# A fused attention and feed-forward kernel: another order and another split of work in its opening

## The reference

```python
h = layernorm(x) * (1 + ca) + sa
q, k, v = h @ Wq.T, h @ Wk.T, h @ Wv.T       # 8 heads, 64 wide for q and k, 128 for v
q, k = rotary(q), rotary(k)                  # x * cos + rotate_half(x) * sin
o = ((q @ k.T) * D**-0.5 * decay_of_head * causal) @ v
o = (o - mean(o)) * rsqrt(var(o) + EPS) * gn_weight + gn_bias      # for each head and token
x = x + ga * ((o * silu(h @ Wg.T)) @ Wo.T)
h = layernorm(x) * (1 + cb) + sb
hp = h shifted by one token
r = sigmoid((mu_r * h + (1 - mu_r) * hp) @ W_r.T)
x = x + gb * r * (relu((mu_k * h + (1 - mu_k) * hp) @ W_k.T) ** 2 @ W_v.T)
```

## Time and profile before

| | |
|---|---|
| median of three runs | 754.27 us (754.24 to 754.61) |
| the profiled execution, its own time | 754.64 us |
| its span from first to last instruction | 752.8 us |
| PE busy | 737.0 us (98%) |
| DVE busy | 605.5 us (80%) |
| POOL busy | 587.6 us (78%) |
| ACT busy | 490.0 us (65%) |

### The profile page before, as it was taken

The page is one execution under the profiler, slowest core; times in us unless marked ns, Lnnn a source line. Parts: engine busy times, 40 slices in busy tenths (PEclk is TensorE's granted clock), DMA queues, the critical chain, the costliest instruction groups (busy, mean ns, idle before and its releaser), DMA issues.

```text
span 752.8 us, 29013 instructions
## 1 busy us (share of the span) xinstructions
PE 737.0 (98%) x12148; PEld 648.1 (86%) x12148; DVE 605.5 (80%) x1272; ACT 490.0 (65%) x953; POOL 587.6 (78%) x642
## 2 busy tenths in 40 slices
PE   6999999999999999999999999999999999999997
PEld 5778888888889889888888988888888988988886
DVE  6988687979888797987879798797988878787546
ACT  3576657566675766767676666756667576666665
POOL 1778778888789887898778888888878987787652
PEclk9999999999999999999999999999999999999999
DMA  9310000000011010111102011020101101001100
GB/s 326 105 38 17 17 17 13 20 17 16 23 30 37 10 44 17 24 37 30 30 10 50 13 27 31 14 47 17 30 23 31 34 13 30 16 10 30 24 15 29
DMA packets 56161, 25.67 MB, mean 34 GB/s; under 512 B 36184, under 2 KB 53856, under 8 KB 56032
## 3 DMA queue, kind: packets, MB, share of 16 engines
q1 hardware_dynamic: 55312, 23.02, 12.8%
q10 hardware_dynamic: 720, 0.80, 0.3%
HBM read 11.22 MB, written 4.20 MB: 20 GB/s over the span
## 4 chain that ended last, share of the span: by engine, by line
PE 93%; issue 2%; POOL 2%; ACT 1%; DVE 1%; DMA 0%; POOLq 0%; DVEq 0%
PE ring L309 53%; PE outs L309 15%; PE O_E L309 13%; PE ring L324 8%; PE O_O L309 3%; PE ring L354 2%; POOL y L1325 1%; ACT y L747 0%; POOL qT L1302 0%; DMA X<-in_x 0%; POOL ln_rstd L1274 0%; POOL gn_rstd L1318 0%; ACT normed L694 0%; ACT v L709 0%; ACT h2T L810 0%
## 5 line engine op out<-in xcount | busy, mean ns | idle before, releaser
L1325 POOL TENSOR_TENSOR y<-y,gate 128x512 f32<-128x512 f32 x123 | 158.9, 1309 | 35.6 <-ACT y L747 35.6
L709 ACT ACTIVATE v<-ring 64x512 f32<-64x512 f32 x128 | 76.1, 594 | 81.4 <-PE ring L309 80.6
L1308 POOL TENSOR_TENSOR rot_k<-rot_k,sin_k 128x256 f32<-128x256 f32 x128 | 106.4, 852 | 24.5 <-DVE sin_k L1028 24.5
L309 PEld LDWEIGHTS outs<-wo_gated,y 128*128 128x128 f32 x992 | 119.7, 192 | 6.7 <-POOL y L1325 2.3
L309 PE MATMUL outs<-wo_gated,y 128*128 128x128 f32 x992 | 121.8, 275 | 1.4 <-POOL y L1325 1.4
L1055 DVE TENSOR_REDUCE gn_sum<-N 128x4 f32<-128x512 f32 x118 | 75.5, 681 | 42.5 <-ACT N L735 42.5
L1318 POOL TENSOR_TENSOR gn_rstd<-gn_var,minus_half 128x8 f32<-128x8 f32 x64 | 105.4, 1646 | 5.0
L1302 POOL TENSOR_TENSOR qT<-qT,swapped 128x512 f32<-128x512 f32 x64 | 82.8, 1294 | 29.1 <-DVE swapped L1011 29.1
L1035 DVE TENSOR_TENSOR A<-ring,consts 128x256 f32<-128x256 f32 x128 | 47.9, 415 | 60.0 <-PE ring L309 60.0
L747 ACT ACTIVATE y<-ring,gn 128x512 f32<-128x512 f32 x126 | 90.9, 776 | 5.1 <-PE ring L324 5.1
L717 ACT ACTIVATE kT<-ring 128x512 f32<-128x512 f32 x64 | 38.3, 598 | 77.7 <-PE ring L324 77.7
(11 more groups left out here) (172 smaller groups left out, 2092.0 us busy)
## 6 DMA issues: line engine op xcount, KB each, us to landing
k_odd<-rot_k SPq DMA_DIRECT2D x128, 64.0 KB, 2.3
X<-in_x SPq DMA_DIRECT2D x16, 256.0 KB, 4.0
out<-X SPq DMA_DIRECT2D x15, 256.0 KB, 2.5
key_tables<-in_const SPq DMA_DIRECT2D x7, 256.0 KB, 8.3
rotary_q<-in_const_q SPq DMA_DIRECT2D x2, 512.0 KB, 8.3
gates<-stored_rows SPq DMA_DIRECT2D x8, 128.0 KB, 3.1
N<-in_w_qkT SPq DMA_DIRECT2D x1, 512.0 KB, 4.7
N<-in_w_vT SPq DMA_DIRECT2D x1, 512.0 KB, 6.0
```

The costliest lines, as they stand in the source:

```text
L309: return e.matmul(o, lhsT, rhs, start=start, stop=stop, skip_group_check=True)
L709: done = e.activation(v[halves(half), i % 2, 1, :, :], by(PAIRS, bank_of["v", odd, i][halves(1 - half), :]), ACT.Copy)
L1308: done = e.tensor_tensor(turned[:, n, :, :], turned[:, n, :, :], sin[:, n, :, :], op)
L1325: e.tensor_tensor(y[:, n % NY, :], y[:, n % NY, :], gate[:, n % 2, :], ALU.mult).then_inc(sem["y"])
```

## The change

It touches the opening alone.

- The queries of group 0 get their rotated partners by a second projection. ACT copies the query weights with quarters exchanged into `mix_k` hi (`round_w_partners`), POOL makes the low part (`low_w_partners`), PE projects both (`project_q_pair`: six products a pair, the partners into the banks of the heads), DVE multiplies each and POOL subtracts. The four shuffles of group 0 go.
- The low part of the query and key weights is made by POOL, no longer by DVE. ACT scales the mean of the value weights, POOL takes it off in two halves (`centre_w_v(odd)`), ACT rounds each half and DVE makes the low part of each (`low_w_v(odd)`). `sum_w_v` stands on DVE ahead of the modulation columns.
- Group 1's statistics, deviation, apply, transpose and modulation stand later on all queues; so do `project_q(4)` and `project_q(5)` on PE, `rotate_q(5)` and `norm_stats(2, 0)` on DVE, `round_w_k` on ACT.
- The filler on PE is 4 narrow and 3 wide calls instead of 12, 15 and 7.
- On SyncE the exchange of chunk 0's keys stands behind the second table load, that of chunk 1 behind the next three loads, and the other loads behind them; `store_gates` comes before the exchange of chunk 2.

```diff
+            def project_q_pair(p):
+                cols = slice(p * P, (p + 1) * P)
+                bank = take_bank(("q", p), ("cos_q", p + 1))
...
+                split_matmul(bank[:, :], [wqk[s][:, cols] for s in ("hi", "lo")], h_parts(0))
+                at.wait_ge("w_partners_lo", 1)
+                at.wait_ge("sin_q", p - 1)
+                bank = bank_of["q_partners", p] = O[p % 2][:, :, :].rearrange("p n v -> p (n v)")
+                split_matmul(bank, [mix_k[s][:, cols] for s in ("hi", "lo")], h_parts(0)).then_inc(sem["proj_q"])
# PE's opening
             mod_columns()
             transpose_n(0, 0)
-            keep_busy(out_bank, 12, False)
-            project_q(0)
-            project_q(1)
-            project_q(2)
-            project_q(3)
+            keep_busy(out_bank, 4, False)
+            project_q_pair(0)
             project_k(0)
+            project_q_pair(1)
+            project_q_pair(2)
             project_v(0, 1)
-            keep_busy(out_bank, 15, True)
+            project_q_pair(3)
             project_v(0, 0)
-            transpose_n(1, 0)
             project_k(1)
-            keep_busy(out_bank, 7, True)
             transpose_k(0)
             project_v(1, 1)
+            keep_busy(out_bank, 3, True)
             scores(0)
             state(0)
-            project_q(4)
             mod_gates()
             project_v(1, 0)
             project_k(2)
+            transpose_n(1, 0)
             transpose_k(1)
             attend(0)
             scores(1)
             recall(0)
             state(1)
-            project_q(5)
+            project_q(4)
             project_v(2, 1)
             project_v(2, 0)
             project_k(3)
+            project_q(5)
             transpose_k(2)
# ACT's opening
             norm_apply(0, 0)
+            round_w_partners()
+            scale_v_mean()
             round_h(0)
-            split_w_v()
+            round_w_v(1)
+            round_w_v(0)
+            split_w_g()
+            copy_v(0, 1)
+            copy_kT(0)
+            copy_v(0, 0)
+            copy_v(1, 1)
             norm_apply(1, 0)
-            copy_v(0, 1)
-            copy_v(0, 0)
-            round_h(1)
-            copy_kT(0)
-            split_w_g()
-            copy_v(1, 1)
             copy_v(1, 0)
             copy_kT(1)
-            round_w_k()
+            round_h(1)
...
# DVE's functions and opening
+            def rotate_q_pair(p):
+                at.wait_ge("const_q0", 16)
+                at.wait_ge("proj_q", p + 1)
+                at.wait_ge("qT", p - 1)
+                e.tensor_tensor((turned, swapped)[p % 2][:, :], bank_of["q_partners", p], rotary_q[:, 1, 0:W], ALU.mult
+                                ).then_inc(sem["sin_q"])
+                e.tensor_tensor(qT[:, 0, p, :], bank_of["q", p][:, :], rotary_q[:, 0, 0:W], ALU.mult).then_inc(sem["cos_q"])
...
             norm_stats(0, 0)
-            split_w("w_qk", raw_qk, wqk)
+            sum_w_v()
             mod_columns()
             full_h(0)
-            sum_w_v()
             low_h(0)
-            centre_w_v()
+            rotate_q_pair(0)
+            rotate_k(0)
+            low_w_v(1)
+            rotate_q_pair(1)
+            low_w_v(0)
+            rotate_q_pair(2)
+            rotate_q_pair(3)
+            rotate_k(1)
             norm_stats(1, 0)
-            rotate_q(0)
-            split_w("w_v", raw_vc, wv)
-            rotate_q(1)
-            rotate_q(2)
-            rotate_k(0)
-            rotate_q(3)
-            full_h(1)
-            rotate_k(1)
-            norm_stats(2, 0)
             mask(0, 1)
             mask(0, 0)
             add_state(0)
+            rotate_k(2)
             mod_gates()
-            rotate_q(4)
-            rotate_k(2)
+            full_h(1)
             mask(1, 1)
             mask(1, 0)
             add_state(1)
-            rotate_q(5)
+            rotate_q(4)
             rotate_k(3)
             norm_heads(0, 0)
             mask(2, 1)
             mask(2, 0)
             norm_heads(0, 1)
+            rotate_q(5)
             add_state(2)
+            norm_stats(2, 0)
             rotate_q(6)
# POOL's functions and opening
+            def low_w_partners():
+                at.wait_ge("w_partners_hi", 1)
+                e.tensor_tensor(with_partners(mix_k["lo"][:, :]), with_partners(raw_qk[:, 0:H * D])[:, :, ::-1, :],
+                                with_partners(mix_k["hi"][:, :]).bitcast(F32), ALU.subtract).then_inc(sem["w_partners_lo"])
+            def centre_w_v(odd):
...
+                at.wait_ge("v_mean", 1)
+                e.tensor_tensor(by(PAIRS, raw_vc[:, cols]), by(PAIRS, raw_v[:, cols]),
+                                v_mean[:, heads].unsqueeze(2).broadcast_to([P, PAIRS, V]), ALU.subtract).then_inc(sem["w_v_centred"])
...
             norm_rstd(0, 0)
+            split_w_qk()
+            low_w_partners()
+            centre_w_v(1)
+            centre_w_v(0)
             rotate_q(0)
-            norm_rstd(1, 0)
+            rotate_k(0)
             rotate_q(1)
             rotate_q(2)
-            rotate_k(0)
             rotate_q(3)
+            rotate_k(1)
+            norm_rstd(1, 0)
+            rotate_k(2)
             low_h(1)
-            rotate_k(1)
             split_w_g()
             rotate_q(4)
-            rotate_k(2)
             head_rstd(0)
             rotate_k(3)
+            rotate_q(5)
             norm_rstd(2, 0)
-            rotate_q(5)
             head_rstd(1)
# SyncE
             load_tables(1)
+            load_tables(2)
+            swap_k(0)
             load_rotary(1)
-            for n in range(2, CB):
-                load_tables(n)
-                if n < NX:
-                    load_x(n)
-            swap_k(0)
+            load_x(2)
+            load_tables(3)
             swap_k(1)
+            for n in range(3, NX):
+                load_x(n)
+                load_tables(n + 1)
+            store_gates()
             swap_k(2)
-            store_gates()
             load_gates(0)
```

More of the change, by code:

```diff
@@ L55 @@
     "v_O", "v_mean", "v_sum", "w_ffn", "w_g", "w_g_hi", "w_g_lo", "w_k_hi", "w_k_lo",
-    "w_mod", "w_o", "w_qk", "w_qk_hi", "w_qk_lo", "w_v", "w_v_centred", "w_v_hi", "w_v_lo", "wffn_v",
+    "w_mod", "w_o", "w_qk", "w_qk_hi", "w_qk_lo", "w_v", "w_v_centred", "w_v_hi", "w_partners_hi", "w_partners_lo", "w_v_lo", "wffn_v",
     "wo_gated", "x0", "x1", "x2", "x3", "x4", "x5", "x6", "y", "zero_column",
@@ L266, in loaded, with with_partners @@
             return "x%d" % (g % NX), 16 * (g // NX + 1)
+        def with_partners(w):
+            return w.rearrange("c (a n q) -> c a n q", n=2, q=QUARTER)
         steps = range(-62, NCHUNK + 5)
@@ L428, in attend @@
                 heads = heads_of(i)
+                at.wait_ge("sin_q", PAIRS)
                 for eo in "EO":
@@ L675, in split_w, with scale_v_mean, round_w_v @@
                 e.activation(parts["hi"][:, :], raw_w, ACT.Copy).then_inc(sem[name + "_hi"])
-            def split_w_v():
-                at.wait_ge("w_v_centred", 1)
-                split_w("w_v", raw_vc, wv)
+            def scale_v_mean():
+                at.wait_ge("v_sum", 1)
+                e.activation(v_mean[:, :], v_mean[:, :], ACT.Copy, scale=1.0 / V).then_inc(sem["v_mean"])
+            def round_w_v(odd):
+                cols = slice(odd * W, (odd + 1) * W)
+                at.wait_ge("w_v_centred", 1 if odd else 2)
+                e.activation(wv["hi"][:, cols], raw_vc[:, cols], ACT.Copy).then_inc(sem["w_v_hi"])
             def split_w_g():
@@ L768, in round_w_k, with round_w_partners @@
                 e.activation(wk["hi"][:, :], wffn[:, 1, :], ACT.Copy).then_inc(sem["w_k_hi"])
+            def round_w_partners():
+                at.wait_ge("w_qk", 16)
+                e.activation(with_partners(mix_k["hi"][:, :]), with_partners(raw_qk[:, 0:H * D])[:, :, ::-1, :], ACT.Copy
+                             ).then_inc(sem["w_partners_hi"])
             def round_mix(g):
+                at.wait_ge("proj_q", PAIRS)
                 at.wait_ge("mix_k", g + 1)
@@ L850, in _ @@
             copy_kT(2)
+            round_w_k()
             scale_norm()
@@ L921, in _, with low_w_v @@
             at = Passed(e)
-            def split_w(name, raw_w, parts):
-                at.wait_ge(name + "_hi", 1)
-                e.tensor_tensor(parts["lo"][:, :], raw_w, parts["hi"][:, :].bitcast(F32), ALU.subtract
-                                ).then_inc(sem[name + "_lo"])
+            def low_w_v(odd):
+                cols = slice(odd * W, (odd + 1) * W)
+                at.wait_ge("w_v_hi", 1 if odd else 2)
+                e.tensor_tensor(wv["lo"][:, cols], raw_vc[:, cols], wv["hi"][:, cols].bitcast(F32), ALU.subtract
+                                ).then_inc(sem["w_v_lo"])
             def sum_w_v():
@@ L1004, in rotate_q @@
                 at.wait_ge("proj_q", m + 1)
-                at.wait_ge("swapped", m)
+                at.wait_ge("qT", PAIRS)
```

(12 more changed lines are left out.)

23 lines of the change are left out of this document (10 added, 13 removed).

## The result

The changed kernel takes 756.6 us (median of 20 runs, 755.0 to 758.03), the kernel before 754.25 on the same chip. The medians differ by 2.35 us. The ratio is 1.0027, 95% interval 1.0021 to 1.0033, which is 2.0 us: slower, and beyond the 0.2% that the prediction counts as no change. The profiled execution took 756.72 us with a span of 754.9 us, where 756.9 and 755.1 were predicted.

What follows compares the result with a forecast made beforehand. DVE up to rotate_q(6) was taken to bound the opening, PE carrying the shift on. 5.1 + 29.8 work + 12.7 holes = 47.6; +2.3 us taken on span 752.8 gives 755.1, median 756.6 us; range 752.9 to 757.9.

Steps and rivals of the forecast that it cites:

- To the first projection: Opening up to PE's first projection: sum_w_v waits for w_v, low_h(0) ends at 12.9, PE starts at 13.0 us, 1.0 earlier.
- low_h(0)'s turn: DVE's low_h(0), ready at 11.05, waits for POOL's centre_w_v(1) at the shared port until 12.2 us; bounds nothing to 1.4.
- the prediction's "only": SBUF port lock at low_h(0): stated as held against a DVE operation with two SBUF inputs only; no size for the word.
- The first pair: PE's first query pair: six products at twice 0.23, 2.7 us, done at 15.8; DVE starts rotate_q(0) at 15.9.
- the rise: PE's clock going from 1.2 to 2.4 GHz: expected after the first pair; if by 13.5 us, 1.2 us less.
- Where the lead goes: From scores(0) to rotate_q(6): 2.8 us lead spent through group 1's norm and head_rstd(0); rotate_q(6) at 47.8, +2.3 us taken.
- DVE's sums: Check over DVE up to rotate_q(6): 29.8 us of work and 12.7 of holes, 47.6 with the start at 5.1.
- Costs set at nothing: Opening: key exchange and later loads on SyncE's queue, gate stores and removed PE filler, each forecast to cost or gain nothing.
- B: Rival for the opening: one early delay absent, POOL's turn or the late clock; +1.2 to +1.4, 755.6 us; chance 0.27.
- D: Rival: faster, the lead at the scores survives, decided by head_rstd(0); 753.6 to 752.6, or 751.5 us; chance 0.15.
- E: Rival: PE's waits between 23 and 50 us let the clock drop again, +1.7 us, 758.3; chance 0.08.

Runs made afterwards that it cites:

- four-moves kernel: Changed kernel with head_rstd(0) directly behind low_h(1), six narrow fillers instead of four, centre_w_v's first half behind low_h(0), full_h(1) ahead of mod_gates: 753.02 us, ratio 0.9984.
- the version with the two moves: Changed kernel with only head_rstd(0) directly behind low_h(1) on POOL and full_h(1) ahead of mod_gates on DVE: 753.79 us, ratio 0.9995.
- the first experiment: Changed kernel with head_rstd(0) on POOL directly behind low_h(1), ahead of split_w_g and rotate_q(4): 755.34 us, ratio 1.0016.
- the version with the old transfers: Changed kernel with SyncE's transfers in the order of the kernel before, store_gates back behind swap_k(2): 756.76 us, ratio 1.0036.
- the two moves with 8 fillers: Changed kernel with head_rstd(0) directly behind low_h(1), full_h(1) ahead of mod_gates and eight narrow fillers instead of four: 753.67 us, ratio 0.9987.
- centre_w_v: Changed kernel in which POOL's first centre_w_v also waits for low_h(0): 756.27 us, ratio 1.0027.

## Why the prediction was right, and where it was not

The measured median is the predicted one, 756.6. The mechanism was right, but that the digits agree is in part luck: the shift of the span was put at 2.3 us and is 2.1, and the median was put 0.37 us below the profiled execution and lies 0.12 below it. The two errors cancel.

**To the first projection: right in kind, two terms too large.** sum_w_v waited for w_v until 7.98 (7.8 forecast), h was rounded at 11.08 (11.0). Splitting the exchanged weights took 1.27 us on POOL, not 1.4: the 16-element groups cost nothing (a plain subtraction of 512 elements takes 1.26). Taking off the mean in halves took 2.04 for both where nothing else was at the port (this is the four-moves kernel, POOL's queue), 1.0 each instead of 1.3, so with the broadcast operand it is cheaper than with a full one:

```profile
9.45 1.28 POOL L1315 TENSOR_TENSOR mix_k_lo<-N,mix_k_hi 128x512 fp32r<-128x512 f32 x1
11.83 2.04 POOL L1323 TENSOR_TENSOR N<-N,v_mean 128x512 f32<-128x512 f32 x2 [1.10 <-DVE hT_lo L1016]
```

So low_h(0)'s turn cost 0.64 us, not 1.2, and PE started at 12.58 instead of 13.0. That it was a turn is shown: with the order at the port settled, the same instruction took 0.69. By the Trainium skill, SBUF — State Buffer, section SBUF: two separate sides, the port pair is held for a whole instruction. The 1.11 to 1.44 us that low_h(0) took in every profile in which POOL came first agree, and so does the gates' operation beside low_h(1) in the version with the two moves: it ended at 33.40, 0.28 us after POOL's. The section also names DVE operations in a two-port mode, which the prediction's "only" leaves out; nothing here rests on that.

**The first pair: right in the sum, the clock longer low than forecast.** The pair was to be done at 15.8, DVE to start at 15.9 after 3.1 us; it was 15.59 after 3.15. But the rise was forecast behind the pair, and the products stayed 0.43 apart to 17.4 us, over five more of them. That cost little, as DVE, not PE, set the pace then: scores(0) came at 25.42, with 25.6 forecast.

**Where the lead goes: right step by step.** full_h(1) ended at 33.0 (33.0), low_h(1) at 35.07 (35.1), project_q(4) started at 35.22 after a wait of 1.24 (35.2, 1.5), head_rstd(0) ended at 41.4 (41.5), norm_heads(0,0) started at 41.46 after 1.83 (41.6, 2.0), rotate_q(6) at 47.52 (47.8). The point that was named as deciding, a head_rstd(0) that ends before 39.7 us, was made true by the first experiment, and the time fell by 1.26 us; with full_h(1) moved too, by 2.8. What the prediction did not say is that 2.0 us of the lead at the scores were only work put off behind them; its sum had that work in the right places (full_h(1) behind the gates' operations, the statistics ahead of rotate_q(6)), so the sum is not touched.

**DVE's sums.** Forecast 29.8 us of work and 12.7 of holes; measured 30.7 and 11.7, where low_h(0)'s 0.64 us of turn counts as work.

**Costs set at nothing.** The exchange of keys and the later loads: nothing, as far as the version with the old transfers can tell. The removal of filler: nothing, as the version with 12 fillers shows, but for another reason than that PE had nothing else to do. It gained a first product 1.3 us earlier and lost the clock's early rise, and the two cancel.

**The rivals.** B, one early delay absent, was priced at 755.6; with the one or the other removed the runs have 756.27 and 756.6. In both profiles rotate_q(6) came 0.75 us earlier, not 1.2, and less than that arrived in the median. D is what the better version does: 753.02, in the 752.6 to 753.6 that D was given, but only with the queue reordered, not as the change stands. E's mechanism did occur, and I had argued that it would not: see the last section. Its 1.7 us of slow products were there (1.6), but they cost under 0.1 us of time.

## What to carry to other kernels

Work that is taken off the fullest engine can be lost again in waits, so follow the chain that ends last through the queues of all engines. Here a small operation whose data was ready (0.3 and 1.65 us on GpSimd) stood in its queue behind a 2.4 us weight split whose result is first used at 63 us, and behind an addition that had to wait; moving that call and one other made 2.8 us. A lead at a landmark counts only after the work that was put off behind it is taken from it: of 3.0 us at the scores, 2.0 were such work. When work is moved to another engine, ask what stands behind it there, and whether it now starts beside an operation of the other engine on the same port.

## What the hardware did that was not expected

**The clock rises later behind a gap.** Where PE went from filler to products without a gap, the products had the full rate (0.23 us apart, 2.4 GHz) from 13.6 to 14.4 us on at the latest (8 fillers, 12 fillers, the four moves, the two moves with 8 fillers). Where it waited 0.62 to 1.58 us in between, they kept, in eight of nine profiles, the rate of 1.2 GHz, 0.43 apart, until 15.7 to 17.5 us. The ninth speaks against a firm rule: with full_h(1) moved, the first product ran at full rate behind a gap of 1.46 us,

```profile
12.32 0.47 PE L312 MATMUL ring<-hT_hi,wqk_hi 128*128 128x512 f32 x1 [1.46 <-DVE hT_lo L1016]
12.63 0.39 PE L312 MATMUL ring<-hT_lo,wqk_hi 128*128 128x512 f32 x1
```

so the gap alone does not settle it. The changed kernel's runs spread more widely than those of the kernel before (755.0 to 758.0 against 753.7 to 755.1 in 18 of 20 runs); how much of that is the clock was not measured.

**And it can fall again in the middle of a busy opening.** In the changed kernel PE ran at half rate, 1.2 GHz, from 44.7 to about 48.1 us (granted clock 0.54, products 0.43 us apart), after waits of 1.24, 1.20 and 0.64 us in the ten us before (busy time by stretches of PE alone, then its queue):

```profile
30.00:44.60 14.60, 11.37 (x272) 1.00 0.58 167
44.60:48.00 3.40, 3.34 (x8) 0.54 0.11 20
48.00:52.00 4.00, 3.88 (x109) 0.97 0.02 4
```

```profile
42.91 0.29 PE L312 MATMUL ring<-v,rot_k 64*64 64x128 f32 x1 [1.20 <-DVE A L1065]
...
44.66 0.65 PE L312 MATMUL ring<-hT_hi,wqk_hi 128*128 128x512 f32 x1 [0.64 <-DVE qT L1038]
45.10 0.63 PE L312 MATMUL ring<-hT_lo,wqk_hi 128*128 128x512 f32 x1
```

Eight products took 0.19 to 0.20 us longer each, some 1.6 us of PE. Yet rotate_q(7) came 6.99 us behind rotate_q(6), where the run with 8 fillers and no fall has 6.92: PE had slack there, so it cost under 0.1 us. Of the thirteen profiles of the changed kernel and its versions five have such a fall (changed, centre_w_v, full_h(1) moved, old transfers, 12 fillers), all with the wait of 1.8 to 2.1 us before norm_heads(0,0); three with that wait have none, and none of the five kernels without it has one. What decides it stays open.
